# Graph layer kernel: the next chunk's transposes placed one by one between the matmuls of two up products

## The chip, the cores and the metric

One Trainium2 chip, one core. The metric is the device time of one execution in microseconds (us); lower is better. TensorE has two clock levels, 1.2 and 2.4 GHz; the profile gives the granted clock as a share of 2.4 GHz.

## The reference

`x` is 50000 x 256 in float32, with 25000 edges. Two layers follow each other. The first adds weighted, normed neighbour rows times `W`. The second is where the change lies:

```python
h = jnp.maximum(_layernorm(x, axis=-1), 0.0)
# inside the second layer (D = 256, hidden 1024)
agg = jax.ops.segment_sum(x[src], dst, num_segments=x.shape[0])
h = agg + x
h1 = h @ W1 + b1
h1 = (h1 - mean) * jax.lax.rsqrt(var + BN_EPS) * gamma + beta
h1 = jax.nn.relu(h1)
out = jax.nn.relu(h1 @ W2 + b2)
# and outside it
x = x + out
```

The kernel knows mean and variance of `h1` before its last stage, from a Gram matrix of `h`.

## The kernel before

The program is written by hand engine by engine, with semaphores; each engine runs its own list in order. Its stages are the two edge stages (up to about 1300 and 1600 us), the Gram stage, and the **node stage** from 1783 us to the end, in which the change lies.

The node stage takes the 50000 nodes in 98 chunks of 512 (128 partitions x 4 rows; the last is 112 x 3). `main_schedule` runs chunk 0, then 24 passes of four chunks in a loop, then the last. In chunk n:

- ScalarE's `prepare` norms four rows of 256 of the chunk's `x` (L625), and VectorE's `add_agg` (L957) adds the aggregate: this is `h`. `prepare(n + 1)` runs after m = 3 of chunk n, `add_agg(n + 1)` after m = 5.
- TensorE transposes `h` in eight 128 x 128 pieces (L1188), four for each half kb of the 256 inputs, into banks 0 and 1 of `ps_a`. ScalarE copies each half, rounded to the matmul type, to `hT_hi` (L668), and VectorE writes the rest to `hT_lo` (L1027).
- For m = 0 to 7 (128 hidden columns each) `up` is six matmuls of 512 columns (L1204) into bank 2 or 3 of `ps_a`: hi x hi, hi x lo and lo x hi for each kb. ScalarE makes `hid` from it (Relu with scale and bias, L677) and `hid_hi` (L682), VectorE makes `hid_lo` (L1035). `down` is four pairs of a matmul of 512 (L1218) and one of 256 columns (L1219) into `ps_b`.
- VectorE reads the four output rows from `ps_b` (L1008, L1011) in two halves, and adds `x` (L1017, `finish`).

On TensorE `down` runs two m behind `up`, and the last two `down` of a chunk stand in the next chunk, behind its transposes. Their order is written in `main` at the end. `up` for m = 0 waits for both halves of `hT_hi` and `hT_lo`; `down` waits for its `hid_lo`; the transposes wait for `h_ready`, which `add_agg` raises.

Of the kernel before, what the change touches and what calls it, by code (L numbers as in the profile page):

```python
def gnn_program(nc, x, src, dst, edge_weight, W, W1, b1, gamma, beta, W2, b2, out):
# [5 lines left out]
    F32, F32R, I32 = mybir.dt.float32, mybir.dt.float32r, mybir.dt.int32  # L28
# [3 lines left out]
    P = 128  # L32
# [42 lines left out]
    with ExitStack() as ctx:  # L75
# [108 lines left out]
        hid_hi, hid_lo = node_r[2:6], node_r[6:10]  # L184

# [140 lines left out]
        def shape_of(n):  # L326

            return (TAIL_P, TAIL_ROWS) if isinstance(n, int) and n == CHUNKS - 1 else (P, ROWS)

        def halves(j):  # L330

            return range(0, 2), range(2, j)
# [213 lines left out]
        def _(act):  # L546
# [99 lines left out]

            def prepare(n, s, k):
                act.wait_ge(norm_picked, CHUNKS + n + 1)
                act.wait_ge(main_loaded[s], 32 * k + 32)
                relu_norm(n, s % 2, s).then_inc(ln_ready, 1)  # L650

# [4 lines left out]

            prepare(0, 0, 0)
            act.wait_ge(bn_pe, 3 + KB)
            act.activation(bn_std[:, :], ps_b[:, 1, 0:MB], ACT.Sqrt, bias=eps_col[:, :]).then_inc(bn_act, 1)

            def main(n, s, k):
                p, j = shape_of(n)
                w = p * j
                for kb in range(KB):
                    act.wait_ge(hT_done, KB * n + kb + 1)
                    act.activation(hT_hi[:, kb, 0:w], ps_a[:, kb, 0:w], ACT.Copy).then_inc(hT_hi_ready, 1)  # L668
                if isinstance(n, int) and n == 0:
                    act.wait_ge(bn_ready, 1)  # L670
                for m in range(MB):
                    act.wait_ge(up_done, MB * n + m + 1)
                    if m >= 2:
                        act.wait_ge(hid_lo_ready, MB * n + m - 1)
                    elif not (isinstance(n, int) and n == 0):
# [3 lines left out]
                    if m >= 4 or not (isinstance(n, int) and n == 0):  # L679
                        act.wait_ge(down_done, MB * n + m - 3)  # L680
                    act.wait_ge(hid_ready, MB * n + m + 1)
                    act.activation(hid_hi[m % 4][:, 0:w], hid[m % 2][:, 0:w], ACT.Copy).then_inc(hid_hi_ready, 1)  # L682
                    if m == 3 and not (isinstance(n, int) and n == CHUNKS - 1):
                        prepare(n + 1, (s + 1) % LOADS, (k if s < LOADS - 1 else k + 1))
            main_schedule(act, main)


        @block.vector
        def _(dve):
# [308 lines left out]
            def read_down(n, s):  # L998
# [3 lines left out]
                for half, rows in enumerate(halves(j)):  # L1002
                    if half == 0:
                        dve.wait_ge(down_half, n + 1)
                    else:
# [6 lines left out]
                                      ALU.add).then_inc(down_read, 1)  # L1012

            def finish(n, s):
                p, j = shape_of(n)
                dve.wait_ge(down_read, 2 * n + 2)
                dve.scalar_tensor_tensor(out_sb[s % 2][0:p, 0:j, :], out_sb[s % 2][0:p, 0:j, :], 0.0, x1_in[s][0:p, 0:j, :],  # L1017
                                         ALU.max, ALU.add).then_inc(out_ready, 1)

            def main(n, s, k):  # L1020

                p, j = shape_of(n)
                w = p * j
                first = isinstance(n, int) and n == 0
                for kb in range(KB):
                    dve.wait_ge(hT_hi_ready, KB * n + kb + 1)
                    dve.tensor_tensor(hT_lo[:, kb, 0:w], ps_a[:, kb, 0:w], hT_hi[:, kb, 0:w].bitcast(F32),  # L1027
                                      ALU.subtract).then_inc(hT_lo_ready, 1)
                if not first:
                    read_down(n - 1, 1 - s % 2)  # L1030
                for m in range(MB):
                    dve.wait_ge(hid_hi_ready, MB * n + m + 1)
                    if m >= 4 or not first:
                        dve.wait_ge(down_done, MB * n + m - 3)
                    dve.tensor_tensor(hid_lo[m % 4][:, 0:w], hid[m % 2][:, 0:w], hid_hi[m % 4][:, 0:w].bitcast(F32),  # L1035
                                      ALU.subtract).then_inc(hid_lo_ready, 1)
                    if m == 1 and not first:
                        finish(n - 1, (s - 1) % LOADS)
                    if m == 5 and not (isinstance(n, int) and n == CHUNKS - 1):
                        add_agg(n + 1, (s + 1) % LOADS, (k if s < LOADS - 1 else k + 1))  # L1040
                    if m == 2 and not (isinstance(n, int) and n + 2 >= CHUNKS):
                        pick_norm(n + 2, s % 2)
# [6 lines left out]
        def _(pe):  # L1049
# [132 lines left out]

            def transpose_h(n, s):
                p, j = shape_of(n)
                pe.wait_ge(h_ready, n + 1)
                for kb in range(KB):
# [4 lines left out]
            def up(n, m):  # L1191
# [6 lines left out]
                if m >= 2 or not (isinstance(n, int) and n == 0):  # L1198
                    pe.wait_ge(hid_ready, MB * n + m - 1)
                cols = slice(m * P, (m + 1) * P)  # L1200
                terms = [(w_part, h_part, kb) for kb in range(KB)
                         for w_part, h_part in ((w1_hi, hT_hi), (w1_hi, hT_lo), (w1_lo, hT_hi))]
# [19 lines left out]
            def main(n, s, k):  # L1222
                transpose_h(n, s)
                if not (isinstance(n, int) and n == 0):
                    down(n - 1, MB - 2)
                    down(n - 1, MB - 1, half=0)
                up(n, 0)
                if not (isinstance(n, int) and n == 0):
                    down(n - 1, MB - 1, half=1)
                up(n, 1)  # L1230
                for m in range(2, MB):
                    up(n, m)
                    down(n, m - 2)
# [23 lines left out]
```

## Time and profile before

| | |
|---|---|
| median of 3 runs (lowest to highest) | 4067.0 us (4066.32 to 4071.11) |
| profiled execution, first to last instruction (its span) | 4058.6 us |
| time outside the span: median less span | 8.4 us |
| busy: PE / PE weight load / DVE / ACT / POOL | 87% / 74% / 54% / 53% / 25% |
| node stage | from 1783 us to the end, 98 chunks |

PE is TensorE's matmuls, PEld its weight loads, DVE is VectorE, ACT ScalarE, POOL GpSimd, SP the engine that issues most DMAs. No total is recorded for the profiled execution other than its span, so the sum is made against the span and 8.4 us are added.

### The profile page before, as it was taken

How to read it: one execution, taken by the hardware profiler on the slowest of the kernel's cores; microseconds unless marked ns; L12 is line 12 of the kernel's file. 1: busy time of each engine (PE TensorE's matmuls, PEld its weight loads, DVE VectorE, ACT ScalarE, POOL GpSimd, SP SyncE). 2: the span in 40 equal slices, each digit the busy share in tenths (PEclk: the TensorE clock that was granted, in tenths of full speed). 3: DMA queues.
4: the chain of work that ended last, by engine and by line, in shares of the span. 5: the costliest groups of instructions: out<-in, count | busy, mean ns of one | idle time of the engine just before them, and what ended most of it. 6: DMA issues, size and time to landing. Idle time of an engine off the chain costs nothing.

```text
span 4058.6 us, 59233 instructions
## 1 busy us (share of the span) xinstructions
PE 3538.1 (87%) x17911; PEld 3016.0 (74%) x17911; DVE 2172.7 (54%) x5226; ACT 2170.4 (53%) x3631; POOL 1034.4 (25%) x801
## 2 busy tenths in 40 slices
PE   0377777677878869999999999999999999999999
PEld 0366666566767657778888888888888888888888
DVE  0255555466666658855545555455555554554554
ACT  0254445332222259956665666656666656566665
POOL 2188888778888820000000000000000000000000
PEclk9788888888888889999999999999999999999999
DMA  7877777567777789932221221212212112122120
GB/s 267 292 168 191 192 172 184 89 162 164 160 162 164 161 255 359 359 133 63 63 76 62 72 68 62 78 62 66 73 62 76 64 62 78 62 68 71 62 78 31
DMA packets 172385, 516.97 MB, mean 127 GB/s; under 512 B 25983, under 2 KB 78202, under 8 KB 166426
## 3 DMA queue, kind: packets, MB, share of 16 engines
q1 hardware_dynamic: 97082, 413.69, 29.9%
q0 software_dynamic: 75264, 102.81, 14.9%
q8 instruction: 18, 0.29, 0.0%
q14 instruction: 21, 0.17, 0.0%
HBM read 361.58 MB, written 206.03 MB: 140 GB/s over the span
## 4 chain that ended last, share of the span: by engine, by line
PE 57%; POOL 20%; issue 10%; DMA 6%; ACT 5%; SPq 1%; DVE 1%; POOLq 0%; ACTq 0%; another core or an unknown queue 0%; DVEq 0%
PE ps_a L1204 27%; PE ps_b L1218 18%; PE ps_b L1219 9%; POOL x_table L510 7%; POOL agg_table L510 7%; POOL arena L504 6%; ACT arena L625 4%; DMA x_table<-in_x 4%; PE ps_a L1188 2%; DMA agg_table<-arena,scatter_now 1%; ACT arena_r L643 1%; SPq L384 1%; DMA x_table<-arena,scatter_now 0%; DMA arena<-in_x,gather_now 0%; PE ps_a L1167 0%
## 5 line engine op out<-in xcount | busy, mean ns | idle before, releaser
L1218 PE MATMUL ps_b<-w_hl,arena_r 128*128 128x512 f32 x3128 | 1140.7, 399 | 0.1
L1035 DVE TENSOR_TENSOR arena_r<-arena,arena_r 128x512 fp32r<-128x512 f32 (+1 forms) x784 | 539.9, 689 | 958.0 <-ACT arena_r L682 958.0
L677 ACT ACTIVATE arena<-ps_a,bn_bias,bn_scale 128x512 f32<-128x512 f32 (+1 forms) x784 | 607.2, 774 | 781.4 <-PE ps_a L1204 781.4
L1204 PE MATMUL ps_a<-arena_r,w_hi 128*128 128x512 f32 x3136 | 982.2, 394 | 1.5 <-DVE arena_r L1027 1.5
L1219 PE MATMUL ps_b<-w_hl,arena_r 128*128 128x256 f32 x3128 | 876.5, 280 | 0.0
L1218 PEld LDWEIGHTS ps_b<-w_hl,arena_r 128*128 128x128 f32 x3128 | 587.5, 188 | 134.5 <-issue 0.4
L1204 PEld LDWEIGHTS ps_a<-arena_r,w_hi 128*128 128x128 f32 x3136 | 540.8, 188 | 109.5 <-ACT arena_r L668 1.9
L1204 PE MATMUL ps_a<-arena_r,w_lo 128*128 128x512 f32 x1568 | 610.9, 390 | 0.0
L1219 PEld LDWEIGHTS ps_b<-w_hl,arena_r 128*128 128x128 f32 x3128 | 589.8, 189 | 26.7
L682 ACT ACTIVATE arena_r<-arena 128x512 fp32r<-128x512 f32 (+1 forms) x784 | 495.1, 631 | 71.6
L742 DVE BATCH_NORM_STATS2 row_stats<-arena 128x6 f32<-128x256 f32 x392 | 137.8, 414 | 562.5 <-DMA arena<-in_x,gather_now 333.4
L1115 PE MATMUL ps_b<-arena,arena_r 128*128 128x256 f32 x1568 | 406.5, 424 | 0.0
L625 ACT ACTIVATE arena<-x_in,norm_now 128x256 f32<-128x256 f32 (+1 forms) x782 | 403.4, 587 | 3.5 <-DVE norm_now L926 3.5
L1104 PE MATMUL ps_b<-wT_hi,arena_r 128*128 128x256 f32 x784 | 215.1, 365 | 196.2 <-DVE arena_r L797 191.9
L1115 PEld LDWEIGHTS ps_b<-arena,arena_r 128*128 128x128 f32 x1568 | 334.8, 217 | 54.1
L510 POOL DMA_INDIRECT x_table<-arena,scatter_now x196 | 318.4, 1624 | 163.0 <-DMA x_table<-in_x 92.2
L1204 PEld LDWEIGHTS ps_a<-arena_r,w_lo 128*128 128x128 f32 x1568 | 295.4, 188 | 67.9
L510 POOL DMA_INDIRECT agg_table<-arena,scatter_now x196 | 318.4, 1624 | 79.1 <-issue 58.2
L1104 PEld LDWEIGHTS ps_b<-wT_hi,arena_r 128*128 128x128 f32 x784 | 177.0, 269 | 200.0 <-DVE arena_r L797 195.0
L575 ACT ACTIVATE arena<-arena,row_norm 128x256 f32<-128x256 f32 x392 | 203.0, 590 | 203.6 <-DVE row_norm L765 185.2
L564 ACT ACTIVATE row_std<-row_moments,eps_col 128x4 f32<-128x4 f32 x98 | 29.1, 297 | 517.7 <-DVE row_moments L751 491.6
L1091 PE MATMUL ps_a<-ones_r,arena_r 128*128 128x2 f32 x980 | 141.7, 269 | 112.3 <-issue 76.5
(118 smaller groups left out, 4302.3 us busy)
## 6 DMA issues: line engine op xcount, KB each, us to landing
x_in<-x_table SPq DMA_DIRECT2D x291, 512.0 KB, 3.8
arena<-agg_table SPq DMA_DIRECT2D x194, 512.0 KB, 5.2
x_table<-in_x SPq DMA_DIRECT2D x10, 5000.0 KB, 31.7
agg_table<-zeros SPq DMA_DIRECT2D x40, 1250.0 KB
out<-zeros SPq DMA_DIRECT2D x97, 512.0 KB, 6.0
arena<-in_x,gather_now POOLq DMA_INDIRECT x196
x_table<-arena,scatter_now POOLq DMA_INDIRECT x196
arena<-x_table,gather_now POOLq DMA_INDIRECT x196
```

Source lines behind the costliest of these rows:

```text
L504: pool.indirect_dma_start(gathered_rows[s][:, a, :], None, l.gather_from, bass.IndirectOffsetOnAxis(ap=gather_now[s][:, a:a + 1], axis=0)) ...
L510: pool.indirect_dma_start(l.scatter_to, bass.IndirectOffsetOnAxis(ap=scatter_now[t.slot(AHEAD)][:, a:a + 1], axis=0), message[t.slot(2)][: ...
L575: ins = act.activation(normed[s][:, a, :], gathered_rows[t.slot(AHEAD)][:, a, :], ACT.Relu, scale=row_norm[s][:, 0, a:a + 1], bias=row_nor ...
L625: ins = act.activation(relu_ln[s][0:p, r, :], x1_in[load][0:p, r, :], ACT.Relu, scale=norm_now[s][0:p, 0, r:r + 1], bias=norm_now[s][0:p, ...
L677: act.activation(hid[m % 2][:, 0:w], ps_a[:, 2 + m % 2, 0:w], ACT.Relu, scale=bn_scale[:, m:m + 1], bias=bn_bias[:, m:m + 1]).then_inc(hid ...
L682: act.activation(hid_hi[m % 4][:, 0:w], hid[m % 2][:, 0:w], ACT.Copy).then_inc(hid_hi_ready, 1)
L1035: dve.tensor_tensor(hid_lo[m % 4][:, 0:w], hid[m % 2][:, 0:w], hid_hi[m % 4][:, 0:w].bitcast(F32), ALU.subtract).then_inc(hid_lo_ready, 1)
L1104: ins = pe.matmul(ps_b[:, 2 * s + b // 2, b % 2 * D:(b % 2 + 1) * D], sums[:, kb, b * P:(b + 1) * P], weight[:, kb, :], start=(i == 0), st ...
L1115: ins = pe.matmul(ps_b[:, 2 * s + b // 2, b % 2 * D:(b % 2 + 1) * D], same[s][:, a, b * P:(b + 1) * P].bitcast(F32), normed[s][:, a, :], s ...
L1204: ins = pe.matmul(ps_a[:, 2 + m % 2, 0:w], w_part[:, kb, cols], h_part[:, kb, 0:w], start=(t == 0), stop=(t == len(terms) - 1))
L1218: pe.matmul(ps_b[0:p, r, :], hid_hi[m % 4][:, cols], w2, start=(m == 0), stop=(m == MB - 1), skip_group_check=True)
L1219: ins = pe.matmul(ps_b[0:p, r, 0:D], hid_lo[m % 4][:, cols], w2[:, 0:D], start=False, stop=(m == MB - 1), skip_group_check=True)
```

## The change

The transposes of chunk n + 1 move from the head of chunk n + 1 into chunk n: the four of half 0 stand in `up(n, 5)`, one behind each of its first four matmuls, those of half 1 in `up(n, 6)`. Since chunk n still reads its own `hT_hi` and `hT_lo` then, there are two buffers of each, picked by the chunk's parity. ScalarE's copies of the halves follow m = 5 and m = 6 of chunk n, VectorE's subtractions too. To have `h` ready earlier, `prepare(n + 1)` moves from behind m = 3 to two halves behind m = 1 and m = 2, and `add_agg(n + 1)` from behind m = 5 to behind m = 3. Chunk 0's own transposes stay ahead of it. No arithmetic changes.

```diff
-        node_r = carve_all(arena_r, *[(KB, CHUNK)] * 2, *[(CHUNK,)] * 8)
-        hT_hi, hT_lo = node_r[0:2]
+        node_r = carve_all(arena_r, *[(KB, CHUNK)] * 4, *[(CHUNK,)] * 8)
+        hT_hi, hT_lo = node_r[0:2], node_r[2:4]
...
+        TRANSPOSE_AT = (5, 6)
...
+            def take_hT(n, s, kb):
+                p, j = shape_of(n)
+                act.wait_ge(hT_done, KB * n + kb + 1)
+                act.activation(hT_hi[s % 2][:, kb, 0:p * j], ps_a[:, kb, 0:p * j], ACT.Copy).then_inc(hT_hi_ready, 1)
...
-                    if m == 3 and not (isinstance(n, int) and n == CHUNKS - 1):
-                        prepare(n + 1, (s + 1) % LOADS, (k if s < LOADS - 1 else k + 1))
+                    if not is_last(n):
+                        if m in (1, 2):
+                            prepare(*following(n, s, k), m - 1)
+                        if m in TRANSPOSE_AT:
+                            take_hT(n + 1, (s + 1) % LOADS, TRANSPOSE_AT.index(m))
...
-                    if m == 5 and not (isinstance(n, int) and n == CHUNKS - 1):
-                        add_agg(n + 1, (s + 1) % LOADS, (k if s < LOADS - 1 else k + 1))
+                    if not is_last(n):
+                        if m == 3:
+                            add_agg(*following(n, s, k))
+                        if m in TRANSPOSE_AT:
+                            hT_low(n + 1, (s + 1) % LOADS, TRANSPOSE_AT.index(m))
...
-            def transpose_h(n, s):
+            def transpose_h(n, s, kb, r):
                 p, j = shape_of(n)
-                pe.wait_ge(h_ready, n + 1)
-                for kb in range(KB):
-                    for r in range(j):
-                        ins = pe.transpose(ps_a[:, kb, r * p:(r + 1) * p], h[s % 2][0:p, r, kb * P:(kb + 1) * P], ident[0:p, 0:p])
+                if kb == 0 and r == 0:
+                    pe.wait_ge(h_ready, n + 1)
+                ins = pe.transpose(ps_a[:, kb, r * p:(r + 1) * p], h[s % 2][0:p, r, kb * P:(kb + 1) * P], ident[0:p, 0:p])
+                if r == j - 1:
                     ins.then_inc(hT_done, 1)
...
                     ins = pe.matmul(ps_a[:, 2 + m % 2, 0:w], w_part[:, kb, cols], h_part[:, kb, 0:w],
                                     start=(t == 0), stop=(t == len(terms) - 1))
+                    if m in TRANSPOSE_AT and not is_last(n) and t < shape_of(n + 1)[1]:
+                        transpose_h(n + 1, (s + 1) % LOADS, TRANSPOSE_AT.index(m), t)
                 ins.then_inc(up_done, 1)
...
             def main(n, s, k):
-                transpose_h(n, s)
-                if not (isinstance(n, int) and n == 0):
+                if is_first(n):
+                    for kb in range(KB):
+                        for r in range(ROWS):
+                            transpose_h(n, s, kb, r)
+                else:
                     down(n - 1, MB - 2)
                     down(n - 1, MB - 1, half=0)
```

The same on TensorE, at the head of a chunk in the loop. Before, the eight transposes (L1188) stand in a block ahead of `down(n - 1, 6)`:

```order
L1218 MATMUL ps_b<-w_hl,arena_r 128x512
L1219 MATMUL ps_b<-w_hl,arena_r 128x256
L344 UNCONDITIONAL_BRANCH
L344 ISA
L1188 MATMUL ps_a<-ident,arena 128x128 x8
L1211 ISA
L1218 MATMUL ps_b<-w_hl,arena_r 128x512
L1219 MATMUL ps_b<-w_hl,arena_r 128x256
```

After the change (the lines have new numbers: L1233 and L1234 are `down`, L1217 is `up`, L1200 a transpose) nothing stands there any more:

```order
L1233 MATMUL ps_b<-w_hl,arena_r 128x512
L1234 MATMUL ps_b<-w_hl,arena_r 128x256
L337 UNCONDITIONAL_BRANCH
L337 ISA
L1233 MATMUL ps_b<-w_hl,arena_r 128x512
L1234 MATMUL ps_b<-w_hl,arena_r 128x256
```

So `down(n - 1, 6)` follows `down(n - 1, 5)` at once. And this is `up(n, 5)` after the change, still on TensorE, with `down(n, 3)` behind it:

```order
L1217 MATMUL ps_a<-arena_r,w1_hi 128x512
L1200 MATMUL ps_a<-ident,arena 128x128
L1217 MATMUL ps_a<-arena_r,w1_hi 128x512
L1200 MATMUL ps_a<-ident,arena 128x128
L1217 MATMUL ps_a<-arena_r,w1_lo 128x512
L1200 MATMUL ps_a<-ident,arena 128x128
L1217 MATMUL ps_a<-arena_r,w1_hi 128x512
L1200 MATMUL ps_a<-ident,arena 128x128
L1217 MATMUL ps_a<-arena_r,w1_hi 128x512
L1217 MATMUL ps_a<-arena_r,w1_lo 128x512
L1233 MATMUL ps_b<-w2_hl,arena_r 128x512
L1234 MATMUL ps_b<-w2_hl,arena_r 128x256
```

Before, these six matmuls of `up` stood together. On ScalarE in a chunk of the loop before, from m = 1 to m = 4, all four rows of `prepare` (L625) stand behind m = 3:

```order
L677 ACTIVATE arena<-ps_a,bn_bias,bn_scale 128x512
L682 ACTIVATE arena_r<-arena 128x512
L672 REGISTER_ALU
L677 ACTIVATE arena<-ps_a,bn_bias,bn_scale 128x512
L682 ACTIVATE arena_r<-arena 128x512
L648 REGISTER_ALU
L649 ISA
L625 ACTIVATE arena<-x_in,norm_now 128x256 x4
L672 REGISTER_ALU
L677 ACTIVATE arena<-ps_a,bn_bias,bn_scale 128x512
```

After the change (L679 for L677, L684 for L682, L646 for L625) two rows stand behind m = 1 and two behind m = 2:

```order
L679 ACTIVATE arena<-ps_a,bn_bias,bn_scale 128x512
L682 REGISTER_ALU
L684 ACTIVATE arena_r<-arena 128x512
L643 REGISTER_ALU
L644 ISA
L646 ACTIVATE arena<-x_in,norm_now 128x256 x2
L676 REGISTER_ALU
L679 ACTIVATE arena<-ps_a,bn_bias,bn_scale 128x512
L684 ACTIVATE arena_r<-arena 128x512
L646 ACTIVATE arena<-x_in,norm_now 128x256 x2
L676 REGISTER_ALU
L679 ACTIVATE arena<-ps_a,bn_bias,bn_scale 128x512
```

Each pair of rows now stands ahead of the Relu of the next m.

## Rows read from the trace of the kernel before

**Rows 1.** The page: busy time, share of the span and instructions of each engine.

```profile
PE 3538.1 (87%) x17911; PEld 3016.0 (74%) x17911; DVE 2172.7 (54%) x5226; ACT 2170.4 (53%) x3631; POOL 1034.4 (25%) x801
```

**Rows 2.** Busy time by window of the node stage.

```profile
core 0: us, PE busy (x) PEld busy (x) DVE busy (x) ACT busy (x) POOL busy (x), PEclk, DMA share, GB/s
2000.00:3000.00 1000.00, 1000.00 (x5180) 849.15 (x5179) 511.09 (x779) 611.10 (x951) 0.00 (x0) 1.00 0.21 68
```

**Rows 3.** Waits, 1810 to 4030 us (us in total, times, longest): the two longest.

```profile
DVE arena_r L1035 <- ACT arena_r L682: 930.6, 574, 2.7
ACT arena L677 <- PE ps_a L1204: 763.3, 575, 2.9
```

**Rows 4.** Busy time by window of one chunk, from transpose block to block.

```profile
3013.56:3036.73 23.17, 23.17 (x123) 19.67 (x122) 11.83 (x18) 14.14 (x23) 0.00 (x0) 1.00 0.21 68
```

**Rows 5.** Timeline of PE and PEld around a transpose block: start, duration, engine, line.

```profile
3013.56 1.03 PE L1188 MATMUL ps_a<-ident,arena 128*128 128x128 f32 x8
...
3014.43 0.19 PEld L1219 LDWEIGHTS ps_b<-w_hl,arena_r 128*128 128x128 f32 x1
3014.67 0.19 PEld L1218 LDWEIGHTS ps_b<-w_hl,arena_r 128*128 128x128 f32 x1
...
3016.54 0.64 PE L1204 MATMUL ps_a<-arena_r,w_hi 128*128 128x512 f32 x2
...
3017.95 0.40 PE L1218 MATMUL ps_b<-w_hl,arena_r 128*128 128x512 f32 x1
```

**Rows 6.** Timeline of PE, the first rows of down(2), up(5) and down(3).

```profile
3026.96 0.39 PE L1218 MATMUL ps_b<-w_hl,arena_r 128*128 128x512 f32 x1
...
3028.36 0.63 PE L1204 MATMUL ps_a<-arena_r,w_hi 128*128 128x512 f32 x2
...
3029.75 0.39 PE L1218 MATMUL ps_b<-w_hl,arena_r 128*128 128x512 f32 x1
```

**Rows 7.** Timeline of PE in the second edge stage; under it the clock there.

```profile
1423.10 1.25 PE L1091 MATMUL ps_a<-ones_r,arena_r 128*128 128x2 f32 x10 [0.79 <-DVE scatter_now L810]
1424.21 7.15 PE L1115 MATMUL ps_b<-arena,arena_r 128*128 128x256 f32 x32
...
1423.10:1427.90 4.80, 4.80 (x27) 4.39 (x28) 3.64 (x13) 3.28 (x6) 3.10 (x2) 1.00 0.66 178
```

**Rows 8.** Timeline of ACT: m = 1, m = 2, then m = 3 and prepare.

```profile
3021.10 0.63 ACT L682 ACTIVATE arena_r<-arena 128x512 fp32r<-128x512 f32 x1
3021.64 0.76 ACT L677 ACTIVATE arena<-ps_a,bn_bias,bn_scale 128x512 f32<-128x512 f32 x1
3022.49 0.63 ACT L682 ACTIVATE arena_r<-arena 128x512 fp32r<-128x512 f32 x1
...
3025.25 0.63 ACT L682 ACTIVATE arena_r<-arena 128x512 fp32r<-128x512 f32 x1
3025.78 2.06 ACT L625 ACTIVATE arena<-x_in,norm_now 128x256 f32<-128x256 f32 x4
```

**Rows 9.** Timeline of DVE, m = 3, then m = 5 with add_agg behind it.

```profile
3025.91 0.69 DVE L1035 TENSOR_TENSOR arena_r<-arena,arena_r 128x512 fp32r<-128x512 f32 x1 [1.48 <-ACT arena_r L682]
...
3031.49 0.69 DVE L1035 TENSOR_TENSOR arena_r<-arena,arena_r 128x512 fp32r<-128x512 f32 x1 [1.52 <-ACT arena_r L682]
3032.10 1.22 DVE L957 TENSOR_TENSOR arena<-arena 128x1024 f32<-128x1024 f32 x1
```

**Rows 10.** Timeline at the stage's start, where PE waits for DVE.

```profile
1785.71 0.69 DVE L1027 TENSOR_TENSOR arena_r<-ps_a,arena_r 128x512 fp32r<-128x512 f32 x1 [0.16 <-ACT arena_r L668]
1786.51 0.50 PEld L1204 LDWEIGHTS ps_a<-arena_r,w_hi 128*128 128x128 f32 x2 [1.88 <-ACT arena_r L668]
```

**Rows 11.** Timeline of m = 7: PE's down(5) after up(7), ACT, DVE.

```profile
3035.32 0.39 PE L1218 MATMUL ps_b<-w_hl,arena_r 128*128 128x512 f32 x1
...
3035.52 0.78 ACT L677 ACTIVATE arena<-ps_a,bn_bias,bn_scale 128x512 f32<-128x512 f32 x1 [1.28 <-PE ps_a L1204]
...
3037.06 0.69 DVE L1035 TENSOR_TENSOR arena_r<-arena,arena_r 128x512 fp32r<-128x512 f32 x1 [2.10 <-ACT arena_r L682]
```

More of the change, by code:

```diff
@@ L328, in shape_of, with is_last, is_first, following @@
             return (TAIL_P, TAIL_ROWS) if isinstance(n, int) and n == CHUNKS - 1 else (P, ROWS)
+        def is_last(n):
+            return isinstance(n, int) and n == CHUNKS - 1
+        def is_first(n):
+            return isinstance(n, int) and n == 0
+        TRANSPOSE_AT = (5, 6)
+        def following(n, s, k):
+            return n + 1, (s + 1) % LOADS, (k if s < LOADS - 1 else k + 1)
         def halves(j):
@@ L645, in _, with prepare @@
             turns(act, CHUNKS, 0, 4, gram)
[L647 to L650, printed above, removed]
+            def prepare(n, s, k, half):
+                p, j = shape_of(n)
+                if half == 0:
+                    act.wait_ge(norm_picked, CHUNKS + n + 1)
+                    act.wait_ge(main_loaded[s], 32 * k + 32)
+                for r in halves(j)[half]:
+                    ins = act.activation(relu_ln[s % 2][0:p, r, :], x1_in[s][0:p, r, :], ACT.Relu,
+                                         scale=norm_now[s % 2][0:p, 0, r:r + 1], bias=norm_now[s % 2][0:p, 1, r:r + 1])
+                if half == 1:
+                    ins.then_inc(ln_ready, 1)
             act.wait_ge(gram_used, CHUNKS + 2)
@@ L672, in main @@
                     act.wait_ge(up_done, MB * n + m + 1)
[L673 to L675 removed]
+                    if m >= 2 or not is_first(n):
                         act.wait_ge(hid_lo_ready, MB * n + m - 1)
@@ L678, in main @@
                                    scale=bn_scale[:, m:m + 1], bias=bn_bias[:, m:m + 1]).then_inc(hid_ready, 1)
-                    if m >= 4 or not (isinstance(n, int) and n == 0):
+                    if m >= 4 or not is_first(n):
                         act.wait_ge(down_done, MB * n + m - 3)
@@ L1012, in read_down, with hT_low @@
                                       ALU.add).then_inc(down_read, 1)
+            def hT_low(n, s, kb):
+                p, j = shape_of(n)
+                dve.wait_ge(hT_hi_ready, KB * n + kb + 1)
+                dve.tensor_tensor(hT_lo[s % 2][:, kb, 0:p * j], ps_a[:, kb, 0:p * j], hT_hi[s % 2][:, kb, 0:p * j].bitcast(F32),
+                                  ALU.subtract).then_inc(hT_lo_ready, 1)
             def finish(n, s):
@@ L1023, in main @@
                 w = p * j
[L1024 to L1029, printed above, removed]
+                first = is_first(n)
+                if first:
+                    for kb in range(KB):
+                        hT_low(n, s, kb)
+                else:
                     read_down(n - 1, 1 - s % 2)
@@ L1197, in up @@
                     pe.wait_ge(hT_lo_ready, KB * n + KB)
-                if m >= 2 or not (isinstance(n, int) and n == 0):
+                if m >= 2 or not is_first(n):
                     pe.wait_ge(hid_ready, MB * n + m - 1)
@@ L1201, in up @@
                 terms = [(w_part, h_part, kb) for kb in range(KB)
-                         for w_part, h_part in ((w1_hi, hT_hi), (w1_hi, hT_lo), (w1_lo, hT_hi))]
+                         for w_part, h_part in ((w1_hi, hT_hi[s % 2]), (w1_hi, hT_lo[s % 2]), (w1_lo, hT_hi[s % 2]))]
                 for t, (w_part, h_part, kb) in enumerate(terms):
@@ L1222, in main @@
             def main(n, s, k):
-                transpose_h(n, s)
-                if not (isinstance(n, int) and n == 0):
+                if is_first(n):
+                    for kb in range(KB):
+                        for r in range(ROWS):
+                            transpose_h(n, s, kb, r)
+                else:
                     down(n - 1, MB - 2)
                     down(n - 1, MB - 1, half=0)
-                up(n, 0)
-                if not (isinstance(n, int) and n == 0):
+                up(n, s, 0)
+                if not is_first(n):
                     down(n - 1, MB - 1, half=1)
-                up(n, 1)
+                up(n, s, 1)
                 for m in range(2, MB):
-                    up(n, m)
+                    up(n, s, m)
                     down(n, m - 2)
```

13 lines of the change are left out of this document (6 added, 7 removed).

## The prediction, as it was put on record

> **What bounds the kernel now.** I read the page first, for the engines' shares: TensorE is busy 87% of the span, VectorE and ScalarE just over half [rows 1]. A share over the whole span says little of one stage, so I asked for windows of the node stage, the only one that the change touches. There TensorE is busy all the time, 1000.00 us of 1000, at a granted clock of 1.00, the higher of its two levels, while ScalarE has 611 and VectorE 511 us of work and the DMAs use a fifth of their time [rows 2]. The waits of this stretch say the same from the other side: ScalarE and VectorE wait for each other and for TensorE's `up`, and no wait of TensorE's is listed [rows 3]. So the stage is TensorE's own stream of matmuls: one chunk takes 23.17 us, all of it busy [rows 4]. A change there pays only by what it takes out of this stream, and costs only by what it adds to it or by a wait that it brings. Moving the transposes to hide their latency can give nothing: no such latency is exposed.
>
> What a measurement of this kernel can tell from no change is about 0.2%, 8.1 us of 4067; spread over the 97 chunks whose transposes move this is 0.084 us a chunk.
>
> **What leaves the stream.** Eight transposes stand in a block from 3013.56; the first matmul behind it has its start where the weight load of the one after it begins, 3014.43 (its own row starts earlier than it can run, for the eighth transpose is not through then). So the block takes 0.87 us, 0.109 each [rows 5]. Behind it the stream runs a trace slower: six pairs of `down` take 2.11 us (3014.43 to 3016.54) and `up(0)` 1.41 (to 3017.95) [rows 5], while elsewhere a `down` of four pairs takes 1.40 and an `up` 1.39 [rows 6]. Six pairs at 1.40 / 4 are 2.10, so some 0.03 go with the block. What leaves is 0.87 to 0.90 us a chunk.
>
> **What enters it.** The same eight transposes, each alone between two matmuls of 512 columns. No row of before shows one alone, so I bound it. Three rows come near. In the block one takes 0.109, with a weight load of its own under the one before [rows 5]. Matmuls of only 2 columns in the edge stage, where nothing but the loads can set the pace, take 0.11 each (1423.10 to 1424.21 for ten, clock 1.00) [rows 7]: that is what a load needs at the least when the instruction before it is short. And matmuls on plain float32, as the transposes are, take 7.15 / 32 = 0.22 for 256 columns [rows 7], thus 0.11 for 128. A lone transpose can hide its own load under the 512 columns before it; but the load of the matmul behind it starts only when the transpose starts, for each load row of the trace begins as the matmul before it begins [rows 5], and that load takes 0.11. So one alone costs 0.11 too, by the load and by its columns alike. The load is merely hidden in another place: eight loads are left uncovered before, eight after. 8 x 0.11 = 0.88 us a chunk, against 0.87 to 0.90 taken out: between -0.02 and +0.01.
>
> From below: if the next load did not count at all and the transpose ran at the pace of the 512-column matmuls, 1.39 / 6 = 0.23 each [rows 6], 128 columns would take 0.058. From above: if each change between the two kinds of matmul cost what the slowest entry beside it shows, 0.02 (0.24 from 3014.43 to 3014.67, against 0.23 [rows 5, 6], and as much again for the transpose), eight would take 8 x 0.13 = 1.04 us. I take 0.11, since three rows of different kinds meet there.
>
> The Trainium skill, "TensorE: Matmul & The Clock Gate", section "Back-to-back issue gap", states for a stream of load and matmul pairs of 128 columns about 81 ns each. By that the eight would take 0.65 us instead of 0.88, and by its rule for LDWEIGHTS, columns over 1.2 GHz, they would take 0.85. The block of this trace, 0.109 each, sides with the second.
>
> **The other engines' edits.** They cost nothing as long as TensorE does not wait; each has to be checked against the moment when TensorE needs it.
>
> *h for the first transpose.* `prepare(n + 1)` now has two rows behind m = 1 and two behind m = 2, each 0.49 on ScalarE ((2.06 - 0.59) / 3). The copy of m = 1 starts at 3021.10, the next item 0.54 later, 3021.64 [rows 8]; there two rows now stand, and the Relu of m = 2 starts at 3022.62. Its copy follows 0.85 later, 3023.47, the next two rows 0.53 after that, and the Relu of m = 3 at 3024.98; its copy at 3025.83, instead of 3025.25 [rows 8]. VectorE's `hid_lo` of m = 3 starts 0.66 behind the copy, 3026.49, `add_agg` 0.61 later at 3027.10, and takes 1.22 [rows 9]: `h` is there at 3028.32. `up(5)` starts at 3028.36 [rows 6], the first transpose 0.23 later, at 3028.59, and its load has to start by 3028.48. From VectorE's end to TensorE's load 0.11 pass (1785.71 + 0.69 = 1786.40, to 1786.51) [rows 10]. So the load can start at 3028.43, 0.05 before it must. That is a thin margin, but a margin. Behind this wait on TensorE's queue stand the rest of `up(5)` and everything else.
>
> *hid_lo of m = 7.* The block stood between `down(5)` and `down(6)` and covered VectorE; now `down(7)` comes 0.87 us sooner. Its `hid_lo` starts 3037.06 - 3035.32 = 1.74 behind the end of `up(7)` and takes 0.69 [rows 11], with the 0.11 that is 2.54. Two `down` at 1.40 less the 0.12 by which a load leads are 2.68. Margin 0.14.
>
> *The rest.* `hT_hi` and `hT_lo` are ready soon after `up(6)`, two `down` and one `up` before they are used. ScalarE gets two copies of 0.6 in m = 5 and 6, where it has over 1 us of idle time a period ([rows 11]: 1.28 waited). The loads of a chunk are issued three chunks ahead, so the earlier `prepare` finds them. The semaphore waits themselves take nothing in this stream.
>
> **The sum.** 97 x (8 x 0.11 - 0.88) is 0, with 97 x (-0.02 to +0.03) = -2 to +3 for roundings. Profiled: 4058.6 + 8.4 outside the span = 4067.0, which is also the median of the runs shown. To that I add 1 us, for a matmul behind a transpose tends to be the slow kind. Forecast 4068.
>
> **The rivals.**
>
> 1. *No change* (the forecast): own range 4064 to 4072. For it: three rows at 0.11. Against it: none shows a transpose alone. Chance 0.64.
>
> 2. *The lone transpose is cheaper*, because the next load overlaps more than the trace has had occasion to show. At the lower bound 8 x (0.109 - 0.058) = 0.41 a chunk, 97 x 0.41 = 40 us: 4027; it is decided for faster once one costs less than 0.099. The Trainium skill's 81 ns (above) would make it 97 x 8 x 0.028 = 22 us, 4045. For it: loads and matmuls do overlap everywhere else. Against it: in ten 2-column matmuls there was nothing else to wait for, and they took 0.11. Chance 0.09.
>
> 3. *Changing kinds costs.* Sixteen times a chunk instead of twice the stream goes from one operand type and bank to the other. At 0.02 for each transpose 97 x 8 x 0.02 = 16 us: 4083. It decides from 0.0105 each. For it: the matmuls behind short ones are the slow ones. Against it: at the block's end there is no gap, 0.109 as within. Chance 0.16.
>
> 4. *h comes late.* If ScalarE's or VectorE's chain runs 0.1 longer than worked out, TensorE waits 0.05 a chunk, 5 us. It decides for slower from 0.13 beyond the chain above: at 0.2 longer, 0.15 x 96 = 14 us, 4082. For it: a margin of 0.05 in 8 us. Against it: all its steps are rows that repeat in every chunk. Chance 0.11, of which 0.08 beyond 0.2%.
>
> **How the numbers follow.** Faster is rival 2, 0.09, and 0.01 of the forecast's edge. Slower is rivals 3 and 4, 0.15 and 0.08, and 0.01 of the edge: 0.24. Same is the rest, 0.66. The predicted time is the forecast's. The range leaves out most of rival 2 and the far ends of 3 and 4: 4056 to 4086.
>
> **What would show it.** Right: between transposes and matmuls in `up(5)` and `up(6)` the load of the matmul behind a transpose starts with the transpose, which takes 0.11; both `up` take 1.39 + 0.44 = 1.83; the chunk stays at 23.17; `down(6)` follows `down(5)` without a gap. Rival 2: `up(5)` well below 1.80. Rival 3: above 1.88, with no wait. Rival 4: a wait of L1200 for `add_agg` in the list of waits, and a gap in PE behind the first matmul of `up(5)`. The prediction is wrong if a load for the matmul behind starts before its transpose does, or if VectorE's hand-over to TensorE takes 0.2 and not 0.11.

## The result, and the profile after

The changed kernel took 4073.0 us (median of 20 runs, 4069.7 to 4076.5), the kernel before 4066.1 us in 20 runs beside it (4063.3 to 4071.1). The ratio is 1.0016, 95% interval [1.0009, 1.0023]: 0.16% slower, 3.7 to 9.4 us. That is clear of zero, inside the range of the prediction, and 5 us above its forecast. The middle of the interval lies inside the 0.2% taken as no change, its upper end (0.23%) a little beyond.

The profiled execution's span is 13.3 us longer than the one of before. Most of that is not the change's: the first transpose starts at 1791.0 us here and at 1783.1 us before, so 7.9 us come from the edge and Gram stages, which the change leaves alone. From the first transpose to the end it is 2280.9 us against 2275.5, 5.4 more. The page's lines that answer to [rows 1], span and busy time of each engine:

```profile
span 4071.9 us, 59279 instructions
PE 3549.6 (87%) x17911; PEld 3002.8 (74%) x17911; DVE 2174.5 (53%) x5226; ACT 2158.2 (53%) x3631; POOL 1034.2 (25%) x801
```

The windows and the waits of the node stage, to set beside [rows 2, 3]:

```profile
2000.00:3000.00 1000.00, 1000.00 (x5168) 839.05 (x5167) 509.03 (x775) 604.00 (x949) 0.00 (x0) 1.00 0.21 68
```

```profile
DVE arena_r L1045 <- ACT arena_r L684: 900.9, 671, 2.7
ACT arena L679 <- PE ps_a L1217: 813.5, 577, 3.5
DVE zeros L1013 <- PE ps_b L1234: 187.2, 192, 1.4
ACT arena_r L684 <- PE ps_b L1234: 4.3, 23, 0.4
PEld ps_a L1200 <- DVE arena L962: 0.2, 1, 0.2
```

TensorE is still busy all the time at full clock, but does 5168 matmuls in the 1000 us instead of 5180. Its only wait is one for `h`, once, 0.2 us (that chunk took 23.33 us, 0.09 more than its neighbours). So nearly all the time was lost inside the stream, in the pace of its matmuls. `up(5)` of one chunk, with `add_agg` (L962) and the weight loads (PEld); L1217 is a matmul of `up`, L1200 a transpose, L1233 the first of `down(3)`:

```profile
3037.91 1.22 DVE L962 TENSOR_TENSOR arena<-arena 128x1024 f32<-128x1024 f32 x1
...
3039.17 0.40 PE L1217 MATMUL ps_a<-arena_r,w_hi 128*128 128x512 f32 x1
3039.19 0.14 PEld L1200 LDWEIGHTS ps_a<-ident,arena 128*128 128x128 f32 x1
3039.41 0.27 PE L1200 MATMUL ps_a<-ident,arena 128*128 128x128 f32 x1
3039.41 0.19 PEld L1217 LDWEIGHTS ps_a<-arena_r,w_hi 128*128 128x128 f32 x1
3039.43 0.48 PE L1217 MATMUL ps_a<-arena_r,w_hi 128*128 128x512 f32 x1
...
3039.54 0.14 PEld L1200 LDWEIGHTS ps_a<-ident,arena 128*128 128x128 f32 x1
3039.75 0.27 PE L1200 MATMUL ps_a<-ident,arena 128*128 128x128 f32 x1
...
3041.01 0.39 PE L1233 MATMUL ps_b<-w_hl,arena_r 128*128 128x512 f32 x1
```

`up(5)` takes 3041.01 - 3039.17 = 1.84 us. The load of the matmul behind a transpose starts with the transpose (3039.41 both), the transpose's own load 0.23 before it, under a long matmul. From a transpose to the next one it is 0.34. A second place lost time too, one where nothing was edited, `up(1)` and `up(2)` together. After the change, first row of `up(1)` and of the `down` behind `up(2)`, 2.79 us:

```profile
3029.41 0.64 PE L1217 MATMUL ps_a<-arena_r,w_hi 128*128 128x512 f32 x2
...
3032.20 0.39 PE L1233 MATMUL ps_b<-w_hl,arena_r 128*128 128x512 f32 x1
```

and the same two places in the kernel before, 2.75 us:

```profile
3018.64 0.63 PE L1204 MATMUL ps_a<-arena_r,w_hi 128*128 128x512 f32 x2
...
3021.39 0.39 PE L1218 MATMUL ps_b<-w_hl,arena_r 128*128 128x512 f32 x1
```

The stream repeats so exactly that it can be summed piece by piece. The table gives each piece's mean over 94 or 95 chunks in ns, from the first matmul of the piece to the first of the next, for the two kernels and the experiments below. "Head" is `down(5)`, the block of transposes where there is one, `down(6)` and the first half of `down(7)`. Most pieces vary by 2 ns or less from chunk to chunk (standard deviation); in the changed kernel, e10 and e11 some vary by 4 to 21 (a chunk of e1 with missing records is left out at `up(0)`).

```
                before  after  e1 none  e2 fours  e4 pairs  e5 eight  e7 grouped  e10 lone+gr.  e11 pairs+gr.
up(1)+up(2)       2747   2782     2783      2783      2783      2783        2747          2747           2747
up(5)             1387   1844     1387      1828      1826      1387        1387          1844           1826
down(3)           1400   1404     1400      1408      1405      1400        1379          1389           1402
up(6)             1387   1842     1387      1842      1828      2262        1387          1840           1837
down(4)           1400   1404     1400      1405      1405      1408        1379          1386           1392
up(7)             1387   1384     1387      1369      1369      1402        1387          1387           1387
head              4390   3516     3520      3520      3520      3525        4359          3490           3490
up(0)             1402   1387     1387      1387      1387      1369        1387          1370           1370
down(7), 2nd       693    690      690       690       690       690         686           686            686
down(0 1 2), up(3 4) 6973 6973    6973      6973      6973      6973        6912          6912           6912
chunk            23167  23227    22313     23206     23187     23200       23013         23053          23050
```

The changed kernel's chunk is 60 ns longer: 918 ns more in `up(5)` to `up(7)`, 892 less in the head, `up(0)` and the half `down`, and 34 more in `up(1)` and `up(2)`. 97 x 0.060 is 5.8 us, in the measured interval.

### The profile page after: what moved, and what is told of

The parts are those of the page before. It is cut to its first block, busy times and chain, and to the rows that moved or that the text cites. A ratio compares the mean times of both kernels' runs of the same rounds, so it can differ in the third digit from the quotient of the medians.

```text
span 4071.9 us, 59279 instructions
## 1 busy us (share of the span) xinstructions
PE 3549.6 (87%) x17911; PEld 3002.8 (74%) x17911; DVE 2174.5 (53%) x5226; ACT 2158.2 (53%) x3631; POOL 1034.2 (25%) x801
## 4 chain that ended last, share of the span: by engine, by line
PE 57%; POOL 20%; issue 10%; DMA 5%; ACT 5%; DVE 1%; SPq 1%; POOLq 0%; ACTq 0%; another core or an unknown queue 0%; DVEq 0%
PE ps_a L1217 27%; PE ps_b L1233 18%; PE ps_b L1234 9%; POOL x_table L503 7%; POOL arena L497 7%; POOL agg_table L503 7%; ACT arena L618 4%; DMA x_table<-in_x 4%; PE ps_a L1200 2%; SPq L377 1%; ACT arena_r L636 1%; DMA x_table<-arena,scatter_now 1%; DMA agg_table<-arena,scatter_now 0%; PE ps_a L1180 0%; DMA arena<-x_table,gather_now 0%
## 5 line engine op out<-in xcount | busy, mean ns | idle before, releaser
L1233 PE MATMUL ps_b<-w_hl,arena_r 128*128 128x512 f32 x3128 | 1129.0, 396 | 0.1
L679 ACT ACTIVATE arena<-ps_a,bn_bias,bn_scale 128x512 f32<-128x512 f32 (+1 forms) x784 | 606.8, 774 | 828.8 <-PE ps_a L1217 828.8
L1217 PE MATMUL ps_a<-arena_r,w_hi 128*128 128x512 f32 x3136 | 1041.8, 410 | 1.5 <-DVE arena_r L1022 1.5
L1234 PE MATMUL ps_b<-w_hl,arena_r 128*128 128x256 f32 x3128 | 876.4, 280 | 0.0
L1233 PEld LDWEIGHTS ps_b<-w_hl,arena_r 128*128 128x128 f32 x3128 | 587.3, 188 | 138.9 <-issue 0.4
L1217 PEld LDWEIGHTS ps_a<-arena_r,w_hi 128*128 128x128 f32 x3136 | 554.5, 188 | 133.6 <-ACT arena_r L666 1.9
L1217 PE MATMUL ps_a<-arena_r,w_lo 128*128 128x512 f32 x1568 | 630.4, 402 | 0.0
L1234 PEld LDWEIGHTS ps_b<-w_hl,arena_r 128*128 128x128 f32 x3128 | 589.7, 189 | 27.5
L684 ACT ACTIVATE arena_r<-arena 128x512 fp32r<-128x512 f32 (+1 forms) x784 | 494.7, 631 | 73.8 <-PE ps_b L1234 4.3
L1217 PEld LDWEIGHTS ps_a<-arena_r,w_lo 128*128 128x128 f32 x1568 | 295.7, 189 | 66.1
L1013 DVE TENSOR_TENSOR zeros<-ps_b,b_bc 128x512 f32<-128x512 f32 x196 | 135.3, 690 | 189.9 <-PE ps_b L1234 189.7
```

The source lines that it names most:

```text
L1233: pe.matmul(ps_b[0:p, r, :], hid_hi[m % 4][:, cols], w2, start=(m == 0), stop=(m == MB - 1), skip_group_check=True)
L1234: ins = pe.matmul(ps_b[0:p, r, 0:D], hid_lo[m % 4][:, cols], w2[:, 0:D], start=False, stop=(m == MB - 1), skip_group_check=True)
```

## The experiments

Eleven kernels ran. Ratios are to the kernel before on the same chip. A chunk's time comes from the one profiled execution of each kernel; where kernels differ by some 20 ns a chunk, the intervals of their ratios overlap, and the order rests on the traces alone.

**e1, no transposes.** The transposes of chunks 1 to 97 are left out, everything else of the changed kernel stays.

```diff
-                    if m in TRANSPOSE_AT and not is_last(n) and t < shape_of(n + 1)[1]:
-                        transpose_h(n + 1, (s + 1) % LOADS, TRANSPOSE_AT.index(m), t)
+                    if m in TRANSPOSE_AT and not is_last(n) and t == 3:
+                        if m == TRANSPOSE_AT[0]:
+                            pe.wait_ge(h_ready, n + 2)
+                        ins.then_inc(hT_done, 1)
```

> The changed kernel with the transposes of chunks 1 to 97 left out (the rows of hT then hold what chunk 0's transposes left in PSUM; ScalarE's and VectorE's work on them stays). It gives the price of the eight transposes in either kernel, follow-up effects included: a chunk takes P0 here, 23.17 us in the kernel before, 23.23 in the changed one. If the block's price is 0.87 to 0.90 us, as I put it, P0 is 22.27 to 22.30 and the time about 3982 us; then the lone ones cost 0.93 to 0.96. If instead something outside the transposes (ScalarE's and VectorE's new order) brought the 0.06 us, P0 is 22.33 to 22.36 and the time about 3988 us.

Measured: 3977.8 us, ratio 0.9796 [0.978, 0.9813], a chunk of 22.313 us. So the block costs 23.167 - 22.313 = 0.854 us a chunk all told, a little less than my 0.87 to 0.90, and the lone transposes 0.914. It also shows where the 34 ns of `up(1)` and `up(2)` do not belong: they are there with no transpose at all, so the lone transposes do not cause them. That the block at the head had spared them is the reading that is left, not one shown by itself, for ScalarE's and VectorE's work on the transposed halves stands at its new place in e1 too, and no run puts it back alone (e5 moves half of it by one m, and the loss stays 34 to 36 ns). e10 below speaks for TensorE's own order. First rows of `up(1)` and of the `down` behind `up(2)`, 2.78 us:

```profile
3016.06 0.64 PE L1217 MATMUL ps_a<-arena_r,w_hi 128*128 128x512 f32 x2
...
3018.84 0.39 PE L1235 MATMUL ps_b<-w_hl,arena_r 128*128 128x512 f32 x1
```

**e2, e4, e5: fours, pairs, one block of eight inside an up product.** The edit of e2; e4 has two behind the second and two behind the fourth matmul, e5 all eight behind the fourth of `up(6)`, with the copies and subtractions of both halves behind m = 6.

```diff
-                    if m in TRANSPOSE_AT and not is_last(n) and t < shape_of(n + 1)[1]:
-                        transpose_h(n + 1, (s + 1) % LOADS, TRANSPOSE_AT.index(m), t)
+                    if m in TRANSPOSE_AT and not is_last(n) and t == 3:
+                        for r in range(shape_of(n + 1)[1]):
+                            transpose_h(n + 1, (s + 1) % LOADS, TRANSPOSE_AT.index(m), r)
```

> The changed kernel with the four transposes of a half in one block behind the fourth matmul of up(5) and of up(6), so 2 places where kinds change instead of 8. Theory A (each lone transpose and the matmul behind it cost some 0.005 more than in a block, since they alternate with long matmuls): up(5) and up(6) fall from 1.84 to about 1.82 us each, and up(1) with up(2) from 2.78 towards 2.75; the chunk takes 23.17 to 23.19. Rival B (a transpose costs the same 0.114 anywhere within an up product, and the alternation is nothing): the chunk stays at 23.23, the time at 4072 to 4073.

> The changed kernel with the transposes two and two, behind the second and the fourth matmul of up(5) and up(6): 4 places where kinds change. Theory A: between the changed kernel and the blocks of four, about 23.20 us a chunk, 4069 us. Rival B: 23.23 us a chunk, as in the changed kernel.

> The changed kernel with all eight transposes in one block behind the fourth matmul of up(6), the copies of both halves behind m = 6. The blocks of four cost more (0.893 a chunk) than the pairs (0.874) and less than the lone ones (0.920), so a rule by the number of places is out. Theory D: a transpose costs 0.108 to 0.110 wherever two or more stand together, and what differs is the pace of the matmuls behind, which goes by how many pairs of `down` stood ahead of them (below, e9). Then up(6) takes 1.387 + 0.87 = 2.26 here, up(1) with up(2) stay at 2.78, and the chunk is between 23.17 and 23.21 us. If the block itself is the cheap thing (0.854 as at the chunk's head), the chunk is at 23.17 and up(1) with up(2) fall to 2.75.

Measured: e2 4065.7 us, 1.0009 [1.0000, 1.0019], 23.206; e4 4063.3 us, 1.0004 [0.9995, 1.0014], 23.187; e5 4066.9 us, 1.0010 [1.0001, 1.0020], 23.200. The lone ones are the dearest, so rival B (no difference) is out: against e1 eight cost 0.914 alone, 0.874 in pairs, 0.893 in fours, 0.887 in one block there, 0.854 at the chunk's head. But the order is not that of the number of places, so theory A is out as I put it too. Pairs beat fours by 19 ns, 14 of them in `up(6)`, which in the fours is 14 ns slower than their own `up(5)` with the same instructions in it. What differs is what ran before. e5 came out as theory D put it: `up(6)` 2.26, `up(1)` with `up(2)` 2.78, the chunk at 23.20; so the block by itself is not the cheap thing.

**e3, only the early `prepare` and `add_agg`** on the kernel before, with `prepare` split in two halves as in the changed kernel.

```diff
-                    if m == 3 and not (isinstance(n, int) and n == CHUNKS - 1):
-                        prepare(n + 1, (s + 1) % LOADS, (k if s < LOADS - 1 else k + 1))
+                    if m in (1, 2) and not (isinstance(n, int) and n == CHUNKS - 1):
+                        prepare(n + 1, (s + 1) % LOADS, (k if s < LOADS - 1 else k + 1), m - 1)
...
-                    if m == 5 and not (isinstance(n, int) and n == CHUNKS - 1):
+                    if m == 3 and not (isinstance(n, int) and n == CHUNKS - 1):
                         add_agg(n + 1, (s + 1) % LOADS, (k if s < LOADS - 1 else k + 1))
```

> The kernel before with only the early prepare (two rows behind m = 1, two behind m = 2) and the early add_agg (behind m = 3); the transposes stay in a block at the chunk's head. If the 0.06 us a chunk come from ScalarE's or VectorE's accesses at new moments (rival C), the chunk takes 23.20 or more here and the time is 4069 or more. If they come from TensorE's own order (theories A and B), it stays at 23.17 and 4066.

Measured: 4061.4 us, 1.0000 [0.9990, 1.0009], a chunk of 23.167, every piece as before to 1 ns. Rival C, the other engines' accesses at new moments, is out for these moves.

**e8, `add_agg` one m later** in the changed kernel (one profiled run).

```diff
-                        if m == 3:
+                        if m == 4:
                             add_agg(*following(n, s, k))
```

> The changed kernel with add_agg one m later on VectorE (behind m = 4). It measures the margin of h: in the changed kernel as it is, TensorE waited 0.2 us in all for h. By my reckoning h then comes about 1.9 us later (the hid_lo of m = 4 at 3028.8 instead of the copy of m = 3's chain), so TensorE waits 1.8 us less some 0.1 a chunk and the chunk takes 24.9 to 25.0 us, 4240 us. If the margin were wide, the chunk would stay near 23.3.

Measured: 4364.6 us. The waits of the stage, and its window:

```profile
...
PEld ps_a L1200 <- DVE arena L962: 205.2, 96, 2.1
DVE zeros L1013 <- PE ps_b L1234: 188.7, 193, 1.4
PE ps_a L1200 <- DVE arena L962: 174.7, 96, 1.8
```

```profile
1810.00:4350.00 2540.00, 2365.19 (x11609) 1955.71 (x11608) 1142.43 (x1739) 1353.70 (x2126) 0.00 (x0) 0.96 0.18 59
```

TensorE's wait is what I worked out, 1.8 us, 96 times, but the chunk takes 26.31 us in the mean instead of 24.9 to 25.0, and against the changed kernel 292 us are lost. Two things were missing. The wait costs more than its length in the list: in the 31 chunks that ran at the higher clock throughout, a chunk takes 25.25 us, 2.03 more than the changed kernel's, and the first transpose starts 2.22 us behind the matmul ahead of it instead of 0.23. And the granted clock is 0.96 over the stage instead of 1.00: in the other 64 of the 95 chunks counted it falls to 1.2 GHz for a stretch, 0.1 to 1.5 us after TensorE has gone on from its wait, and these take 26.83 us, 1.57 more. 96 x 2.03 + 64 x 1.57 = 295, against 292 measured. A wait that recurs costs more here than its own length. The trace also gives the hand-over: the load starts 0.05 us after `add_agg` ends, in all 96 chunks.

**e7, grouped `down`** on the kernel before: the four long matmuls of a `down` first, then its four short ones.

```diff
-                for r in (range(j) if half is None else halves(j)[half]):
-                    cols = slice(r * p, (r + 1) * p)
-                    pe.matmul(ps_b[0:p, r, :], hid_hi[m % 4][:, cols], w2, start=(m == 0), stop=(m == MB - 1), skip_group_check=True)
-                    ins = pe.matmul(ps_b[0:p, r, 0:D], hid_lo[m % 4][:, cols], w2[:, 0:D], start=False, stop=(m == MB - 1), skip_group_check=True)
+                rows = range(j) if half is None else halves(j)[half]
+                for r in rows:
+                    pe.matmul(ps_b[0:p, r, :], hid_hi[m % 4][:, r * p:(r + 1) * p], w2, start=(m == 0), stop=(m == MB - 1), skip_group_check=True)
+                for r in rows:
+                    ins = pe.matmul(ps_b[0:p, r, 0:D], hid_lo[m % 4][:, r * p:(r + 1) * p], w2[:, 0:D], start=False, stop=(m == MB - 1), skip_group_check=True)
```

> The kernel before with each `down` written as its 512-column matmuls first and its 256-column ones behind them, instead of pair by pair. A `down` of four pairs takes 1.400 now: 227, 232, 241, 236 ns for the long and 113, 117, 120, 113 for the short ones. If the alternation of long and short makes the long ones slow, the long ones fall to 227 and the `down` to about 1.37, and the `up` behind it to 1.36: 8 x 0.03 + 8 x 0.02 = 0.4 us a chunk, 4025 us. If the short ones are held by their loads when they stand together (0.11 to 0.12), little changes: 4060 to 4070.

Measured: 4047.8 us, 0.9963 [0.9950, 0.9976]: faster than the kernel before by 0.4%, clear of zero. A `down` and the `up` behind it:

```profile
3014.17 1.07 PE L1218 MATMUL ps_b<-w_hl,arena_r 128*128 128x512 f32 x4
3015.07 0.64 PE L1220 MATMUL ps_b<-w_hl,arena_r 128*128 128x256 f32 x4
3015.55 0.63 PE L1204 MATMUL ps_a<-arena_r,w_hi 128*128 128x512 f32 x2
...
3016.93 0.39 PE L1218 MATMUL ps_b<-w_hl,arena_r 128*128 128x512 f32 x1
```

The long ones run at 3015.07 - 3014.17 = 0.90 for four, 0.225 each by these rounded starts (227 expected), the short ones at 0.12, the `down` is 1.38 instead of 1.40. The `up` behind it still takes 1.38 to 1.39, so 0.154 of the 0.4 us a chunk that I expected came. 97 chunks at 0.154 less are 15 us.

**e9, pairs, and `down(7)` not split** around `up(0)`.

```diff
                     down(n - 1, MB - 2)
                     down(n - 1, MB - 1, half=0)
+                    down(n - 1, MB - 1, half=1)
                 up(n, s, 0)
-                if not is_first(n):
-                    down(n - 1, MB - 1, half=1)
                 up(n, s, 1)
```

> The kernel with pairs of transposes (e4), and `down(7)` not split around up(0): twelve pairs of `down` in a row, then up(0), up(1), up(2) together. In the traces so far the pace of an `up` goes by the number of pairs ahead of it: after 4 or 10 pairs its six take 1.387, after 2 pairs 1.402 and the next up 1.381, and after a run that ends as a third or sixth pair does (241, 120 ns) 1.371. Theory D says that twelve pairs end like that, so up(0) takes 1.371, up(1) and up(2) 1.362 each, 4.095 instead of 4.170, and the chunk 23.11 to 23.12 us: 97 x 0.07 = 7 us less than e4, 4056 against 4062 of the kernel before. If the pace goes by something else, the chunk stays at 23.19.

Measured: 4063.0 us, 1.0002 [0.9993, 1.0011], a chunk of 23.167. First rows of `up(0)`, of `down(0)` behind `up(2)`, and of `up(3)`; under them a wait of this kernel's list:

```profile
3019.73 0.62 PE L1217 MATMUL ps_a<-arena_r,w_hi 128*128 128x512 f32 x2
...
3023.82 0.44 PE L1234 MATMUL ps_b<-w_hl,arena_r 128*128 128x512 f32 x1
...
3025.26 0.39 PE L1217 MATMUL ps_a<-arena_r,w_hi 128*128 128x512 f32 x1
```

```profile
PEld ps_b L1234 <- issue: 19.0, 92, 0.2
```

The forecast of the pace came true: the three `up` take 4.09 us, against 4.17 in two pieces, seventeen of the eighteen matmuls at 227 ns. But 0.04 us were given back at `down(0)`, 1.44 us instead of 1.40, where a load is now held in 92 chunks, and 0.02 in the twelve pairs; 4056 was forecast. The list says only "issue", but the trace shows what the load waited for. VectorE's `hid_lo` of m = 0 and that load:

```profile
3023.01 0.69 DVE L1045 TENSOR_TENSOR arena_r<-arena,arena_r 128x512 fp32r<-128x512 f32 x1 [0.97 <-ACT arena_r L684]
...
3023.77 0.19 PEld L1234 LDWEIGHTS ps_b<-w_hl,arena_r 128*128 128x128 f32 x1 [0.21 <-issue]
```

`hid_lo` ends at 3023.70. In all 96 chunks the load starts 0.07 after that end, also in the first few, where it is held for 0.01 to 0.02 less; in e4 it starts 0.34 after it, with the matmul ahead. So `down(0)` has come too early for its `hid_lo`, since the half `down` that stood between `up(0)` and `up(1)` is gone: a wait, and not the pace. The pace rule holds, the sum did not.

**e10, e11: grouped `down` on the changed kernel and on the pairs.** The edit is that of e7.

> The changed kernel with each `down` written as its 512-column matmuls first, its 256-column ones behind. The same edit on the kernel before gave a chunk of 23.013 us, in which an up product takes 1.387 behind any `down` and up(1) with up(2) 2.747. If the 0.034 us that up(1) and up(2) lost in the changed kernel came from how the pairs before them ended (theory D), it is gone here: up(1) with up(2) take 2.75. The lone transposes keep their price, up(5) and up(6) take 1.84. Chunk 23.00 to 23.04 us, 4046 to 4050 us. If the 0.034 belongs to the removal of the block whatever the order in `down`, up(1) with up(2) stay at 2.78.

> The same with the transposes two and two (e4). In e4 up(5) and up(6) took 1.826 and 1.829 where the lone ones took 1.844 and 1.842. Then the chunk is 0.03 shorter than in e10, 22.97 to 23.01 us, 4043 to 4047 us: at best level with, or a little ahead of, the block at the chunk's head with the same `down` (4048).

Measured: e10 4055.4 us, 0.9972 [0.9962, 0.9981]; e11 4054.9 us, 0.9970 [0.9959, 0.9981]. `up(1)` and `up(2)` are back at 2747 ns, as theory D said, with the lone transposes in place: that loss hangs on how the short matmuls ahead are arranged. The lone ones keep their 1.84. The size was missed in both: e10's chunk is 23.053 instead of 23.00 to 23.04, e11's 23.050 instead of 22.97 to 23.01, since `down(3)` and `down(4)` do not stay at e7's 1.379 (1.389 and 1.386 in e10, 1.402 and 1.392 in e11). The times, 4055 each, are above their forecasts too (4046 to 4050, 4043 to 4047); some 2 us of that are the chip's, on which the kernel before took 4065.8 and not 4063.4 as beside e7. Against e7 the change now costs 0.040 us a chunk, with pairs 0.037.

**e12, a matmul of 2 columns in place of each moved transpose** (one profiled run); the transposes of chunks 1 to 97 are left out.

```diff
...
+                        small = pe.matmul(ps_a[:, TRANSPOSE_AT.index(m), 2 * t:2 * t + 2], w1_hi[:, 0, t * P:(t + 1) * P], ones_r[:, 0:2],
+                                          start=True, stop=True)
...
```

> The changed kernel with each moved transpose replaced by a matmul of 2 columns at the same place, with a weight load of 128 columns of its own (w1_hi); the transposes of chunks 1 to 97 are left out. It asks what sets the 0.11 us. If the load of the matmul behind sets it (theory L, what I put first), a 2-column matmul costs the same: up(5) and up(6) stay at 1.82 to 1.85, the chunk at 23.2. If the transpose's own 128 columns on float32 set it (theory S), up(5) falls towards 1.387 + 4 x 0.03 = 1.50, the chunk to 22.55, 4005 us.

Measured: 4068.9 us, a chunk of 23.175. `up(5)` of one chunk; L1222 is the small matmul, L1238 the first of `down(3)`:

```profile
3012.08 0.40 PE L1217 MATMUL ps_a<-arena_r,w_hi 128*128 128x512 f32 x1
...
3012.32 0.16 PE L1222 MATMUL ps_a<-ones_r,w_hi 128*128 128x2 f32 x1
3012.32 0.19 PEld L1217 LDWEIGHTS ps_a<-arena_r,w_hi 128*128 128x128 f32 x1
...
3012.43 0.19 PEld L1222 LDWEIGHTS ps_a<-ones_r,w_hi 128*128 128x128 f32 x1
...
3013.93 0.40 PE L1238 MATMUL ps_b<-w_hl,arena_r 128*128 128x512 f32 x1
```

`up(5)` takes 1.85 us in this chunk, 1.84 in the mean, with 2 columns as with 128. The load of the matmul behind begins at 3012.32, with the small matmul, and the one after it 0.11 later. Theory S (the columns) is out: a short matmul between long ones costs as much as the load of the matmul behind it. The small matmul is also of the same operand type as its neighbours, so a change of type is not what is paid for either. One rival stays: a fixed price of 0.11 for each load with its matmul, however short, would look the same, and no run has a short matmul with no load behind it.

## Why the prediction was right, and where it was off

*TensorE's stream is the bound, and no wait takes its place.* Right: busy 1000 us of 1000, one wait of 0.2 us in the stage.

*The lone transpose costs the load behind it, 0.11.* That the transpose's own columns do not set the price is shown by e12, and in the loads' rows the load behind starts with the transpose; a fixed price for each load with its matmul is not excluded. The Trainium skill, "TensorE: Matmul & The Clock Gate", section "LDWEIGHTS (loading the stationary operand)", gives columns over 1.2 GHz, 107 ns for 128; the 0.11 of e12 agrees. The Trainium skill's 81 ns for pairs of 128 columns (same page, section "Back-to-back issue gap") is met nowhere here, and rival 2 with it. One of the three rows on which the 0.11 rested was misread: where the edge stage issues 16 matmuls on plain float32 (L1115) the trace has 32 records [rows 7], so 256 columns there take two records of 0.22 and not one, and the row does not give 0.11 for 128 columns. The other two rows hold. The size was a little off: `up(5)` and `up(6)` rose by 912.6 ns for eight, 0.114 each instead of 0.11, and with the `down` behind them the term "8 x 0.11 = 0.88" measured 0.918. By its size that is 0.005 each, where rival 3 had 0.02 and would have decided from 0.0105. Its mechanism did not show: e2, e4 and e5 are not in the order of the number of changes, and e12 has no change of operand type and still pays 0.113 each in `up(5)` and `up(6)`. What the 0.005 are stays open.

*What leaves is 0.87 to 0.90.* The head, `up(0)` and the half `down` gave back 0.892.

*Missing from the sum:* 0.034 us in `up(1)` and `up(2)`, where nothing was edited. I had seen that the stream behind the block runs slower and booked 0.03 as a gain from its removal, which came. I did not ask how the pieces after those would start. e1 shows that the loss is there without any transpose, e10 that it goes when `down` is grouped. It is more than half of the 60 ns. The sum's own allowance, -0.02 to +0.03 a chunk, did not hold it, and its +0.03 was more than the +0.01 that the terms ahead of it gave. The forecast of no change held because what was missed, 0.060, is under the 0.084 that counts as a change; it held with little room.

*h comes 0.05 before it must.* In the chunk shown it came earlier than that: `add_agg` ends at 3037.91 + 1.22 = 3039.13, the load starts at 3039.19, and it had until 3039.41 - 0.11 = 3039.30. The chain of rows was right to 0.01; the hand-over was too long, at most 0.06 there and 0.05 in e8, not the 0.11 of the stage's start. The argument against rival 4, that the chain's rows repeat in every chunk, was wrong: in 22 of 96 chunks `h` came some 0.08 later against `up(5)`, the load started 0.10 behind the matmul ahead instead of 0.02, and only 0.02 of the margin was left (`up(5)` took 1.847 there instead of 1.842). Once it was too late: the one wait of 0.2. Rival 4 thus came in one chunk, for 0.09 us. e8 shows what it costs when it recurs, 3 us a chunk for a wait of 1.8.

*hid_lo of m = 7, margin 0.14.* No wait appeared. `hid_lo` ends 0.26 before the load that needs it starts, 1.14 in the kernel before; with a hand-over of 0.05 to 0.07 some 0.2 were left.

## What to carry to other kernels

Moving short matmuls between long ones hides their own loads but uncovers as many others: on a stream bound by TensorE, count for each short matmul the load behind it (0.11 us here), wherever it stands. And when work is taken out from ahead of a matmul, check the margin of what that matmul waits for, as in e9. The gain lay elsewhere, in the order of long and short matmuls that were there already: grouping equal lengths gave 0.4% with an edit of a few lines. And where a stream has no waits, sum it piece by piece over a whole period in both traces, for pieces that nobody edited can change.

## What was not expected of the hardware

The pace of equal matmuls depends on what ran before them, to the nanosecond and in every chunk. Six matmuls of `up` with the same operands take 1387 ns behind four or ten pairs of `down`, 1402 behind other arrangements, 1369 behind others again. In a row of long ones they settle at 227 ns each, after five in the kernel before and ten in the changed one; in e9, where twelve pairs stood ahead, all but the first ran at 227. The changed kernel's chunks differ among themselves (23.175 to 23.240 us from `up(1)` to `up(1)`, but for the one with the wait) and repeat every 12 chunks, three passes of its loop. A rule in the number of pairs foretold e9's pace, but what in the chip keeps this memory stays open: no run here separates loads, operand reads and instruction supply.

In e8 a wait of 1.8 us in a chunk of about 26 brought the granted clock to 1.2 GHz for 8% of the stage; waits of 0.2 us or less (e9) left it at its higher level.
